# Attention with a leaky slope: one parametric ReLU and one exponential on ScalarE in place of two exponentials and a maximum on VectorE

## The reference

```python
h = relu(layernorm(x));  A = (adj != 0)
for i in range(3):                       # block 1
    aggr = A^T @ (h @ weight[i])
    h = gru_cell(aggr, h, w_ih, w_hh, b_ih, b_hh)
x = x + h
h = relu(layernorm(x)) @ W^T             # block 2
f_i, f_j = h @ a[:128], h @ a[128:]
e = f_i[:, None] + f_j[None, :]
e = where(e >= 0, e, 0.2 * e)            # the leaky slope
att = softmax(where(adj > 0, e, -9e15), axis=2)
x = x + att @ h
```

## Time and profile before

| What | Value |
|---|---|
| median of 3 runs | 503.27 us (502.77 to 505.48) |
| the profiled execution, its own time | 503.9 us |
| its span, first to last instruction | 502.1 us |
| PE busy | 460.3 us, 92% of the span |
| DVE busy | 441.2 us, 88% |
| ACT busy | 359.6 us, 72% |
| POOL busy | 140.5 us, 28% |
| mean granted TensorE clock | 0.985 |

### The profile page before, as it was taken

One profiled execution on the slowest core, in us unless ns is written; L12 is line 12 of the kernel. 1 busy time (PEld: TensorE's weight loads), 2 busy tenths in 40 slices (PEclk: granted clock), 3 DMA queues, 4 the chain that ended last, 5 costly groups with the idle time before them and its releaser, 6 DMA issues. The chain is left out here.

```text
span 502.1 us, 8215 instructions
## 1 busy us (share of the span) xinstructions
PE 460.3 (92%) x2547; PEld 375.1 (75%) x2547; DVE 441.2 (88%) x1087; ACT 359.6 (72%) x641; POOL 140.5 (28%) x170
## 2 busy tenths in 40 slices
PE   4799997999999999999999999999999999998575
PEld 2476776787878878887878878787888878786465
DVE  3768889999999999999999999899999999887844
ACT  3364765687959688796968778795968778676374
POOL 2114244332412233332312333232213333131500
PEclk9989999999999999999999999999999999999979
DMA  6620030110303030030303021030303000000001
GB/s 178 209 85 0 2 101 3 41 67 22 106 21 106 23 102 4 27 101 21 106 22 105 22 65 41 22 106 22 104 23 105 1 23 1 22 1 22 22 1 42
DMA packets 26746, 26.34 MB, mean 52 GB/s; under 512 B 840, under 2 KB 18512, under 8 KB 26704
## 3 DMA queue, kind: packets, MB, share of 16 engines
q1 hardware_dynamic: 26704, 25.83, 15.9%
HBM read 21.63 MB, written 4.19 MB: 51 GB/s over the span
## 5 line engine op out<-in xcount | busy, mean ns | idle before, releaser
L1122 PE MATMUL X<-A_ring,nat_hi 128*128 128x512 f32 x192 | 78.8, 411 | 2.2 <-DVE A_ring L712 2.0
L1122 PE MATMUL X<-A_ring,nat_lo 128*128 128x512 f32 x192 | 76.3, 398 | 0.0
L852 DVE SCALAR_TENSOR_TENSOR prob<-e 128x512 f32<-128x512 f32 x64 | 61.4, 959 | 13.8 <-ACT e L467 13.8
L1240 PE MATMUL G<-hp,probT 128*128 128x128 f32 x512 | 67.5, 275 | 0.7 <-issue 0.7
L285 POOL TENSOR_TENSOR hT_lo<-hT,hT_hi 128x512 fp32r<-128x512 f32 x19 | 25.4, 1334 | 150.5 <-ACT hT_hi L393 134.1
L1240 PEld LDWEIGHTS G<-hp,probT 128*128 128x128 f32 x512 | 63.2, 192 | 2.2 <-issue 0.9
L466 ACT ACTIVATE e<-g,nb 128x512 f32<-128x512 f32 x64 | 46.6, 729 | 5.8 <-DVE nb L845 5.8
L443 ACT ACTIVATE gn<-npre,vecs 128x512 f32<-128x512 f32 x48 | 34.6, 721 | 16.0 <-DVE npre L770 15.6
L467 ACT ACTIVATE e<-g,nb 128x512 f32<-128x512 f32 x64 | 45.9, 717 | 0.0
L1122 PEld LDWEIGHTS X<-A_ring,nat_hi 128*128 128x128 f32 x192 | 36.6, 191 | 11.3 <-issue 2.6
L473 ACT COPY probT<-G 128x512 f32<-128x512 f32 x64 | 37.4, 584 | 10.3 <-PE G L1229 10.2
(11 more groups left out here) (136 smaller groups left out, 1205.4 us busy)
## 6 DMA issues: line engine op xcount, KB each, us to landing
adj_raw<-in_adj SPq DMA_DIRECT2D x16, 1024.0 KB, 5.6
x_ring<-in_x SPq DMA_DIRECT2D x16, 256.0 KB, 2.9
out_x<-out_sb SPq DMA_DIRECT2D x16, 256.0 KB, 2.2
wih_in<-in_L_gnn_w_ih SPq DMA_DIRECT2D x1, 192.0 KB, 3.1
wl_in<-in_L_gnn_weight SPq DMA_DIRECT2D x1, 192.0 KB, 4.1
whh_in<-in_L_gnn_w_hh SPq DMA_DIRECT2D x1, 192.0 KB, 4.2
w_in<-in_L_gnn_W SPq DMA_DIRECT2D x1, 64.0 KB
vec_in<-in_L_gnn_b_ih SPq DMA_DIRECT2D x1, 1.5 KB
```

The source lines that it names most:

```text
L852: dve.scalar_tensor_tensor(out=prob[:, c], in0=e1[:, c % 2], scalar=1.0, in1=e2[:, c % 2], op0=ALU.mult, op1=ALU.max, accum_out=psums[:, k ...
L1122: mm = pe.matmul(X[:], part[s][:, c], A_ring[:, (k - s) % RING, c], start=(c == 0 and part is nat_hi), stop=(c == C - 1 and part is nat_lo))
L1240: mm = pe.matmul(G2[:, c * D:(c + 1) * D], probT[:, c % 2, j], hp[:, (k + 1) % 2, j, 0:D], start=(j == 0), stop=(j == C - 1))
```

## The change

DVE's maximum goes. In its place ACT makes a parametric ReLU of slope 5 on the negated score, in place in `g`: with `hp` now holding -f_i, it computes y = -(g + f_i) where that is positive, and 5 times it elsewhere. One exponential with scale -0.2 then yields exp of the leaky score, and its row sum comes from ACT's accumulator output. The two biases become one, `nguard`. The buffers e1 and e2 go; ACT writes `prob` itself, which has four chunks.

```diff
-            def exps(i, k, c):
+            def leaky(i, k, c):
                 if on(i, GB):
                     if c == 0:
-                        act.wait_ge(nb_done, (i - (GB - 1)) * 2)
-                    if c >= 2:
-                        act.wait_ge(prob_done, (i - GB) * C + (c - 1))
-                    act.activation(e1[:, c % 2], g[:, k % 2, c], ACT.Exp, bias=nb1[:, k % 2, c:c + 1])
-                    act.activation(e2[:, c % 2], g[:, k % 2, c], ACT.Exp, bias=nb2[:, k % 2, c:c + 1], scale=SLOPE).then_inc(exp_done, 1)
+                        act.wait_ge(hp_done, i - (GB - 1))
+                    act.wait_ge(g_done, (i - GB) * C + (c + 1))
+                    act.activation(g[:, k % 2, c], g[:, k % 2, c], ACT.Prelu, bias=hp[:, (k + 1) % 2, c, D:D + 1],
+                                   scale=-1.0, alpha=1.0 / SLOPE).then_inc(lr_done, 1)
+
+            def exps(i, k, c):
+                if on(i, GB):
+                    if c == 0:
+                        act.wait_ge(guard_done, i - (GB - 1))
+                    act.wait_ge(lr_done, (i - GB) * C + (c + 1))
+                    act.activation(prob[:, c], g[:, k % 2, c], ACT.Exp, bias=nguard[:, k % 2, c:c + 1], scale=-SLOPE,
+                                   accum_out=psums[:, k % 2, c:c + 1]).then_inc(prob_done, 1)
...
-                dve.tensor_copy(wT[:, D:D + 2], Z[:, 0:2]).then_inc(wa_done, 1)
+                dve.tensor_scalar(wT[:, D:D + 1], Z[:, 0:1], -1.0, None, ALU.mult)
+                dve.tensor_copy(wT[:, D + 1:D + 2], Z[:, 1:2]).then_inc(wa_done, 1)
...
-                    dve.tensor_tensor(top[:], hp[:, (k + 1) % 2, :, D], gmax[:, k % 2], ALU.add).then_inc(top_done, 1)
-                    dve.wait_ge(top_done, i - (GB - 1))
-                    dve.scalar_tensor_tensor(out=ltop[:], in0=top[:], scalar=SLOPE, in1=top[:], op0=ALU.mult,
-                                             op1=ALU.max).then_inc(ltop_done, 1)
...
+                    dve.tensor_tensor(ntop[:], hp[:, (k + 1) % 2, :, D], gmax[:, k % 2], ALU.subtract).then_inc(ntop_done, 1)
+                    dve.wait_ge(ntop_done, i - (GB - 1))
+                    dve.scalar_tensor_tensor(out=nguard[:, k % 2], in0=ntop[:], scalar=SLOPE, in1=ntop[:], op0=ALU.mult,
+                                             op1=ALU.min).then_inc(guard_done, 1)
-            def probabilities(i, k, c):
-                if on(i, GB):
-                    dve.wait_ge(exp_done, (i - GB) * C + (c + 1))
-                    dve.scalar_tensor_tensor(out=prob[:, c], in0=e1[:, c % 2], scalar=1.0, in1=e2[:, c % 2],
-                                             op0=ALU.mult, op1=ALU.max, accum_out=psums[:, k % 2, c:c + 1]).then_inc(prob_done, 1)
```

More of the change, by code:

```diff
@@ L137, in graph_block @@
         gmax = sb("gmax", [P, 2, C])
[L138 to L143, removed]
+        ntop = sb("ntop", [P, C])
+        nguard = sb("nguard", [P, 2, C])
         prob = sb("prob", [P, C, N])
@@ L188, in graph_block @@
         h2_turned, h2T_done, fj_mm, hp_mm = (sem(n) for n in ("h2_turned", "h2T_done", "fj_mm", "hp_mm"))
-        hp_done, g_done, top_done, ltop_done, nb_done = (sem(n) for n in ("hp_done", "g_done", "top_done", "ltop_done", "nb_done"))
-        exp_done, prob_done, prob_turned, probT_done = (sem(n) for n in ("exp_done", "prob_done", "prob_turned", "probT_done"))
+        hp_done, g_done, ntop_done, guard_done, lr_done = (sem(n) for n in ("hp_done", "g_done", "ntop_done", "guard_done", "lr_done"))
+        prob_done, prob_turned, probT_done = (sem(n) for n in ("prob_done", "prob_turned", "probT_done"))
         att_mm, rsum_done, out_done = sem("att_mm"), sem("rsum_done"), sem("out_done")
@@ L481, in full @@
                 normed(i, k)
+                leaky(i, k, 0)
+                neighbours_high(i, k, 1)
+                leaky(i, k, 1)
                 exps(i, k, 0)
-                neighbours_high(i, k, 1)
                 exps(i, k, 1)
                 turned_prob(i, k, 0)
+                leaky(i, k, 2)
                 first_state_high(i, k)
                 exps(i, k, 2)
+                leaky(i, k, 3)
                 candidate(i, k, 2)
@@ L587, in _ @@
             neighbours_high(16, 0, 2)
+            leaky(16, 0, 0)
+            leaky(16, 0, 1)
             exps(16, 0, 0)
@@ L590, in _ @@
             reset_gate(16, 0, 2)
+            leaky(16, 0, 2)
             exps(16, 0, 1)
@@ L595, in _ @@
             neighbours_high(16, 0, 1)
+            leaky(16, 0, 3)
             exps(16, 0, 2)
@@ L610, in _ @@
             neighbours_high(17, 1, 2)
+            leaky(17, 1, 0)
+            leaky(17, 1, 1)
             exps(17, 1, 0)
+            leaky(17, 1, 2)
             exps(17, 1, 1)
@@ L614, in _ @@
             turned_prob(17, 1, 0)
+            leaky(17, 1, 3)
             exps(17, 1, 2)
@@ L623, in _ @@
             values(17, 1)
+            leaky(18, 2, 0)
+            leaky(18, 2, 1)
             exps(18, 2, 0)
             attention_input(18, 2)
+            leaky(18, 2, 2)
             exps(18, 2, 1)
             values(18, 2)
+            leaky(18, 2, 3)
             exps(18, 2, 2)
@@ L632, in _ @@
             turned_prob(18, 2, 2)
+            leaky(19, 3, 0)
+            leaky(19, 3, 1)
             exps(19, 3, 0)
             turned_prob(18, 2, 3)
+            leaky(19, 3, 2)
             exps(19, 3, 1)
             turned_prob(19, 3, 0)
+            leaky(19, 3, 3)
             exps(19, 3, 2)
@@ L876, in full @@
                 natural_high0(i, k)
-                probabilities(i, k, 0)
                 neighbours_low(i, k, 1)
                 adjacency(i, k)
-                probabilities(i, k, 1)
                 before_tanh(i, k, 2)
@@ L883, in full @@
                 x2_stats(i, k)
-                probabilities(i, k, 2)
                 x2_mean(i, k)
@@ L891, in full @@
                 neighbours_low(i, k, 0)
-                probabilities(i, k, 3)
                 mask(i, k)
@@ L1015, in _ @@
             neighbours_low(16, 0, 2)
-            probabilities(16, 0, 0)
             natural_low(16, 0, 1)
@@ L1021, in _ @@
             x2_stats(16, 0)
-            probabilities(16, 0, 1)
             neighbours_low(16, 0, 1)
@@ L1025, in _ @@
             renew(16, 0, 2)
-            probabilities(16, 0, 2)
             x2_mean(16, 0)
@@ L1030, in _ @@
             before_tanh(16, 0, 1)
-            probabilities(16, 0, 3)
             keep(16, 0, 1)
@@ L1040, in _ @@
             residual(17, 1)
-            probabilities(17, 1, 0)
             x2_stats(17, 1)
-            probabilities(17, 1, 1)
             reset(17, 1, 2)
-            probabilities(17, 1, 2)
             x2_mean(17, 1)
             before_tanh(17, 1, 2)
-            probabilities(17, 1, 3)
             keep(17, 1, 2)
@@ L1057, in _ @@
             offsets(18, 2)
-            probabilities(18, 2, 0)
-            probabilities(18, 2, 1)
             scores(19, 3)
-            probabilities(18, 2, 2)
             offsets(19, 3)
-            probabilities(18, 2, 3)
-            probabilities(19, 3, 0)
-            probabilities(19, 3, 1)
             output(18, 2)
-            probabilities(19, 3, 2)
-            probabilities(19, 3, 3)
             output(19, 3)
```

## The result

The kernel is slower: 508.01 us median (506.13 to 508.72, 10 runs) against 503.3 us, ratio 1.0079, 95% interval [1.0065, 1.0094]. The difference is under 1%, but clear of the noise. The forecast was 499.6 us; the time lies above the range, on the side that the second and the third rival had spoken for.

What follows compares the result with a forecast made beforehand. PE was taken as the bound in steady iterations, busy 332 of 342 us. Twelve iterations gave -0.7 us and the tail -3.0, together -3.7, so 499.6 us from the median 503.27; range 495 to 507.5.

Steps and rivals of the forecast that it cites:

- the second and the third rival: DVE's collision with POOL moves: 503.2 us, no change, 27%; ACT's chain dearer by 0.1 us per step: 507.3 us, 18%.
- DVE's relief: Steady iterations: without the maxima PE no longer waits for DVE, winning at most 1.04 us per iteration.
- the sign of being wrong: Steady part: an iteration below 28.0 us or above 28.8, or a tail still taking 72 us, would refute the prediction.
- Price of ACT's new work: On ACT: each parametric ReLU steps 0.62 us like an exponential; the accumulator read steps 0.10, between 0.07 and 0.16.
- The rival of dearer ACT steps: ACT's chain: each new ReLU or read costs 0.1 us more than taken, giving 507.3 us; chance 18%.
- that of the tables: On ACT: the parametric ReLU needs another function table, six loads per iteration, the kernel 120 us more; chance 1%.
- Where the new order waits: ACT between agg_hi and first_state: its longer chain makes PE late at the first transposes and at neighbours of step 0.
- 0.78 + 2a: PE's loss in us at neighbours of step 0 per iteration, with 0.10 us taken for each accumulator read's step.
- The collision: POOL's second-norm passes beside hT_lo, fresh and rv on DVE: some 0.3 us reach PE per iteration, 503.2 us; chance 27%.
- per iteration -0.26 + 2a: Steady iteration: PE's loss to ACT's chain less 1.04 us won; -0.06 us with each read at 0.10, -0.7 over twelve.
- The tail: After the steady iterations: waits for DVE's maximum and a slow instruction go, nine reads cost 0.9; sum -3.0 us.

Runs made afterwards that it cites:

- e3: Changed kernel, steady iterations: on DVE the second norm's statistics and mean moved ahead of agg_lo of step 1; 502.51 us, ratio to before 0.998.
- e1: Changed kernel, steady iterations: on ACT the ReLU of chunk 1 moved ahead of neighbours_high of step 1; 503.5 us, ratio to before 1.0001.
- e2: Changed kernel, steady iterations: on ACT the ReLU of chunk 3 moved behind first_state, right ahead of its exponential; 503.82 us, ratio to before 1.0017.
- e6: Changed kernel with the moves of e1 and e2 together; 497.33 us, ratio to before 0.9866.
- e4: Changed kernel with the row sum left out everywhere, sums set to 1 once, output not normalised; 506.32 us, ratio to before 1.0064.
- e7: Changed kernel with the edits of e3 and e4 together; 498.69 us, ratio to before 0.9903.
- e5: Changed kernel with the moves of e1, e2 and e3 together; 488.16 us, ratio to before 0.9699.
- b1: Kernel before the change, with the edit of e3; 500.28 us, ratio to before 0.9935.

## Why the prediction was wrong

**What bounds the kernel, and DVE's relief: right.** PE's idle time per iteration was the right thing to count. The stretch that ends with `project` went from 7.06 to 6.03 us on the mean, 1.03 won, where 1.04 was forecast. But an iteration of 29.01 us is above the 28.8 that was named as the sign of being wrong, and DVE is busy 400 us and not 375; 16 of these 25 us are hT_lo and fresh, lengthened by the collision below.

**Price of ACT's new work: right.** The ReLU takes 720 ns on the mean and its step is 0.62. The step of the read is 0.09, forecast 0.10. There is no second table load. The rival of dearer ACT steps is out, and so is that of the tables. That the first of them named 507.3 us, close to the measured time, is luck: none of its steps is dearer.

**Where the new order waits: right place, too small.** PE was to start `neighbours` of step 0 by 0.78 + 2a = 0.98 us later; it is, on the mean, 0.65 - 0.17 + 0.75 = 1.23, some 0.24 more. The wrong term is the hand-over from ACT to PE, 0.06 us in the earlier trace rows, used twice. Here the read ends at 159.90 and PE starts at 160.04, 0.14; of these 0.08 more, 0.04 are left at `first_state`, which starts 6.23 us after agg_hi where 6.19 was forecast. hT ends at 164.79 and the matmul starts at 165.04, 0.25, which is 0.19 more. The row that I took the 0.06 from stands before transposes in the tail. The weight load of the matmul starts at 165.01, so the time passes ahead of the load and not in it; what it is spent on was not tried and stays open.

**The collision: the step that failed.** The sum "per iteration -0.26 + 2a" has no term for it. I had it as a rival at 0.3 us with DVE's slack taking the rest, and counted it as nothing in the forecast, though the maximum that took 1.40 us was in the earlier trace rows and the rival itself puts POOL's two passes beside hT_lo, fresh and rv. It cost 0.32 us in the changed kernel (1.13 against 0.81), shown by e3, which takes it away and changes nothing on ACT, and 0.65 in e1, e2 and e6. The Trainium skill, "SBUF — State Buffer", section on the two separate sides, has it that a DVE instruction with two SBUF inputs and a GpSimd instruction that reads SBUF exclude each other, and that the one that starts second waits for the whole of the first. Each of these rows agrees: the caught instruction reads two SBUF tiles and ends some 0.55 us after POOL's pass, whichever it is, and npre, with one tile from PSUM, is not caught.

Forecast and difference in sum, per iteration and on the means: -0.06, +0.24 for the hand-overs, +0.32 for the collision, +0.01 at `project`, -0.02 in the first stretch: +0.49, which is what the means differ by. Over twelve iterations the collision is 3.9 us and the hand-overs 2.9.

**The tail: the sum right, its terms not.** -2.9 us, forecast -3.0. The instruction of the last gated step that took 1.53 us takes 0.69 again, as forecast:

```profile
474.91 0.69 DVE L811 SCALAR_TENSOR_TENSOR fresh<-tz,gn 128x512 f32<-128x512 f32 x1
```

But the accumulator reads cost 0.3 to 0.4 us (69.4 in e4 and e7, which have none, against 69.7 and 69.8 in the changed kernel and e3) and not 0.9. So what went was worth 3.2 to 3.3 us and not 3.9; PE's waits for DVE's maximum, 3.1 us, became in part waits for ACT's copy to probT. That the sum fits is in part luck.

**The sum.** 12 x 0.49 - 2.9 = +3.0 us is what steady iterations and tail explain. The medians differ by 4.7 us; the ratio of 1.0079 is 4.0, between 3.3 and 4.7. So 1.0 to 1.7 us are left. The only other stretch is the filling, below; that they lie there is not shown.

## What to carry to other kernels

Where an engine is nearly full, count what a change opens and closes in the in-order list of that engine, and price every new wait with a hand-over seen ahead of the same instruction where the trace has one. Removing work from an engine that shares something with another can move the meeting and not end it, as it did here: look up what runs beside the other engine's passes afterwards. And a change of engines needs its order redone: the same instructions, with three moves in their order, went from 0.8% slower to 3.0% faster.

## What was not expected of the hardware

The filling of the pipeline has the same instructions in the changed kernel and in e1, e2, e3, e5 and e6, yet the first `project` started at 89.00, 85.67 (e1), 86.65 (e2), 86.09 (e3), 88.12 (e6), 87.22 (e5) and, in the changed kernel again, at 87.37. With one small instruction more it was 86.00 (e4) and 88.35 (e7), and in the kernel before 87.23 and 85.95 (b1). The window of 12 to 36 us, length, busy times by engine, then granted clock (third from the end), of the changed kernel:

```profile
12.00:36.00 24.00, 19.01 (x63) 13.86 (x64) 16.63 (x37) 10.25 (x21) 4.30 (x5) 0.79 0.36 116
```

and of e1:

```profile
12.00:36.00 24.00, 19.80 (x76) 14.21 (x76) 17.71 (x41) 12.04 (x22) 4.28 (x5) 0.93 0.44 154
```

The clock stands longer at its lower level, 1.2 GHz, in the first. There PE idled 1.8 us for `A_ring` up to 13.69, and from 14 to 18 us the granted clock was 0.60 and 0.55; it fell again behind a second idle stretch, at 24 us. In e1 PE idled 1.2 us at the first of these places, the clock stayed at 1.00, and it fell only behind the second. As the same instructions start `project` anywhere from 85.67 to 89.00, the 1.8 us of the profiled execution are not the change's instructions. Whether the changed kernel draws the long filling more often than the one before, which would explain the 1.0 to 1.7 us that are left, stays open: the mean granted clock, which every execution left, is 0.9865 over 16 executions of the changed kernel and 0.9861 over 47 of the one before, and does not tell them apart.
